# 16-bit one-hots with the keys innermost, in the counting loop of an edge sort and in the fetch of target values

## Chip, cores and metric

The program runs on one core of a Trainium2 chip. The metric is the device time of one execution in microseconds, the median of several runs. The engines named below are PE (TensorE; PEld are its weight loads), DVE (VectorE), ACT (ScalarE), POOL (GpSimd) and SP (SyncE, which here only issues transfers).

## What is computed

A stack of four graph layers over 6250 nodes and 100,000 edges, each with a residual and a layer norm. Two places matter here. The edges are sorted by their source node, and a spline convolution moves each edge's coordinates by a value fetched at its two end nodes:

```
row, col = (edge_index[0], edge_index[1])
deg = jax.ops.segment_sum(jnp.ones_like(msg[:, 0]), row, num_segments=N)
...
new_pseudo = jnp.clip(pseudo + t[col] - t[row], 0.0, 1.0)
basis2, idx2 = spline_basis(new_pseudo)
```

## The kernel before

Edges lie as 128 partitions by J = 784 columns. Each edge has a key (a node number below 6272), which is split into a low digit (key modulo 128) and a high digit (key divided by 128, below NT = 49). Gathers and counts over keys are made with one-hot matrices: for a column of 128 keys, `hot_lo` is 128 x 128 (is the low digit n?) and `hot_hi` is 128 x 49. A matmul of the two counts how many of the 128 keys equal each node number.

**stage_rank** sorts the edges. DVE first splits the keys into digits. Then come two loops of 28 iterations, two steps each.
- The counting loop (`v.Fori(0, steps)` at L402 on DVE, L502 on PE): in each of 56 steps DVE makes the one-hots of ST = 14 key columns (`make`: copy 28 digits to PSUM at L374, `hot_lo` at L377, `hot_hi` at L379), into one of two buffers, and PE adds 14 matmuls to `table` (L507) and then frees the buffer (`hot_free`).
- After a short piece on DVE (L412 to L395) the ranking loop, again of 56 steps, makes the same one-hots once more, finds each edge's place, and POOL scatters the edges to `sorted` (L564), 14 scatters for each step. DVE may overwrite the buffer `at`/`rows` only when `rank_free` has been raised, and SP raises it when it has seen that buffer's scatters land (L575).
- SP's program in this stage begins with `load_constants`: 49 transfers that clear `adj` (L279), then the loads of the weights and constants (L282). Its loop on `rank_free` stands behind these in SP's order.

**stage_targets** fetches t[col] for all edges. Steps of CH = 28 key columns, 28 steps in a loop. In each, DVE makes the one-hots of the next step (L1761, L1764, L1766), and then picks the values of this one in `units` = 7 units of 4 columns (multiply at L1777) and sums them (L1784). PE for each unit adds 4 matmuls to `counts` (L1827), turns 4 `hot_lo` into rows (L1828), ACT copies these out of PSUM (L1816), and PE looks up the values with 12 matmuls (L1838) into one of two `found` buffers, which DVE frees after its pick. POOL meanwhile works off a share of another scatter (L1086, `scatter_pairs`).

All one-hots are bf16 with the key outermost, `[P, keys, digits]`, so that the matrix of one key column is contiguous. The digits they are compared with, and the row of numbers `iota`, are f32, and the digits lie in PSUM.

## Time and profile before

| | us |
|---|---|
| median of 3 runs (12901.63 to 12932.95) | 12922.68 |
| profiled execution, its own time | 12949.96 |
| its span | 12948.2 |
| counting loop | about 44 to 256 |
| ranking loop | about 274 to 1562 |
| stage_targets, its loop | about 5481 to 6567 |

Over the span PE is busy 26%, DVE 43%, ACT 19%, POOL 52%. Such shares are means over some fifty stages that run one after another, so each stage is to be read by itself.

### The profile page before, as it was taken

How to read it: one execution, taken by the hardware profiler on the slowest of the kernel's cores; microseconds unless marked ns; L12 is line 12 of the kernel's file. 1: busy time of each engine (PE TensorE's matmuls, PEld its weight loads, DVE VectorE, ACT ScalarE, POOL GpSimd, SP SyncE). 2: the span in 40 equal slices, each digit the busy share in tenths (PEclk: the TensorE clock that was granted, in tenths of full speed). 3: DMA queues.
4: the chain of work that ended last, by engine and by line, in shares of the span. 5: the costliest groups of instructions: out<-in, count | busy, mean ns of one | idle time of the engine just before them, and what ended most of it. 6: DMA issues, size and time to landing. Idle time of an engine off the chain costs nothing. (4 is left out here: it accounts for less than half of the span.)

```text
span 12948.2 us, 84897 instructions
## 1 busy us (share of the span) xinstructions
PE 3406.5 (26%) x19713; PEld 2120.5 (16%) x19713; DVE 5568.4 (43%) x7052; ACT 2481.3 (19%) x3625; POOL 6758.2 (52%) x6784
## 2 busy tenths in 40 slices
PE   2344301773333333402410001000100010005877
PEld 1222200331111111302410001000100010004544
DVE  7333385445444445302755442222322277774111
ACT  0222143332222222100100000111111134440000
POOL 0666566006666666573047766776677656651000
PEclk9555555885555555555755555555555555557899
DMA  6000022786777777300036641111111123335899
GB/s 269 2 3 3 12 89 76 292 336 208 233 233 236 235 233 229 93 0 0 0 100 185 176 137 32 33 35 29 32 34 32 29 63 99 95 96 172 325 385 362
DMA packets 587391, 1693.59 MB, mean 131 GB/s; under 512 B 268075, under 2 KB 322770, under 8 KB 569201
## 3 DMA queue, kind: packets, MB, share of 16 engines
q0 software_dynamic: 292720, 608.23, 18.5%
q1 hardware_dynamic: 230560, 722.30, 14.4%
q10 hardware_dynamic: 63952, 361.30, 7.3%
q8 instruction: 56, 0.92, 0.0%
q14 instruction: 103, 0.84, 0.0%
HBM read 1016.07 MB, written 675.24 MB: 131 GB/s over the span
## 5 line engine op out<-in xcount | busy, mean ns | idle before, releaser
L1979 POOL DMA_INDIRECT ring<-tab_gat,at x2352 | 2350.8, 999 | 920.5 <-issue 837.5
L710 POOL DMA_INDIRECT ring<-z_stn,at x1568 | 1512.5, 965 | 1530.6 <-POOLq L707 1034.8
L710 POOL DMA_INDIRECT ring<-z_conv,at x784 | 802.0, 1023 | 890.1 <-POOLq L707 628.1
L564 POOL DMA_INDIRECT sorted<-rows,at x784 | 801.2, 1022 | 776.1 <-POOLq L562 542.8
L1503 PE MATMUL pair_acc<-pair_w,pair_cell 32*112 32x384 f32 (+1 forms) x1120 | 788.4, 881 | 1545.7 <-issue 519.8
L1086 POOL DMA_INDIRECT adj<-val_a,at_a x784 | 780.3, 995 | 334.9 <-issue 255.7
L2558 PE MATMUL acc<-spot,ones 128*128 128x128 f32 x6 | 2.3, 486 | 3440.4 <-PEq L2549 1195.5
L1253 PE MATMUL acc<-tile,parts 128*96 128x448 f16 (+1 forms) x3430 | 730.5, 362 | 254.8 <-DVE parts L1177 138.7
L1898 DVE COPY corner_banks<-w 128x56 f32 (+1 forms) x140 | 35.6, 255 | 1579.8 <-issue 448.7
L2090 DVE COPY peak<-peak 128x6 f32<-128x6 f32 x112 | 20.9, 187 | 1562.2 <-DMA ring<-tab_gat,at 1498.7
L1503 PEld LDWEIGHTS pair_acc<-pair_w,pair_cell 32*112 32x112 f32 x1120 | 315.6, 296 | 2017.4 <-issue 2017.4
L2558 PEld LDWEIGHTS acc<-spot,ones 128*128 128x128 f32 x6 | 1.5, 312 | 3441.1 <-issue 3441.1
L2126 DVE TENSOR_TENSOR_SCAN sums<-decay,sums 128x1176 f32<-128x1176 f32 (+1 forms) x112 | 517.3, 4619 | 29.0 <-issue 12.2
L1540 ACT COPY pair_block<-pair_acc 112x384 f32<-112x384 f32 (+1 forms) x896 | 380.0, 501 | 749.3 <-issue 374.5
L1253 PEld LDWEIGHTS acc<-tile,parts 128*96 128x96 bf16 (+1 forms) x3430 | 404.9, 125 | 574.3 <-DMA tile<-adj 238.4
L2014 ACT ACTIVATE weights_bank<-arg 128x168 f32<-128x168 f32 (+1 forms) x112 | 31.2, 279 | 2410.0 <-issue 1953.1
L2113 DVE TENSOR_TENSOR sums<-ring,weights_bank 128x1008 f32<-128x1008 f32 (+1 forms) x112 | 430.0, 3839 | 145.9 <-issue 109.4
L1159 POOL DMA_INDIRECT own<-tab_gcn,ex_src x5 | 5.0, 990 | 905.1 <-DMA tab_gcn<-hop 602.4
L2029 ACT COPY out_rows<-sums 128x1176 f32<-128x1176 f32 (+1 forms) x112 | 443.0, 3955 | 49.0 <-ACTq L2028 15.9
L1623 PE MATMUL planes<-wsb,turned 64*128 64x384 f32 (+1 forms) x1960 | 421.9, 537 | 72.9 <-PEq L1619 72.9
L1777 DVE TENSOR_TENSOR prod<-found,hot_hi 128x588 f32<-128x588 f32 x196 | 151.1, 771 | 622.9 <-remote 300.5
L822 DVE TENSOR_TENSOR_SCAN sums<-decay,sums 128x448 f32<-128x448 f32 (+2 forms) x168 | 387.8, 2308 | 43.2 <-issue 24.2
(503 smaller groups left out, 9709.3 us busy)
## 6 DMA issues: line engine op xcount, KB each, us to landing
tile<-adj SPq DMA_DIRECT2D x490, 784.0 KB, 21.4
z_stn<-block ACTq DMA_DIRECT2D x245, 800.0 KB, 4.9
z_conv<-pair_block ACTq DMA_DIRECT2D x224, 700.0 KB
run_gat<-out_rows SPq DMA_DIRECT2D x56, 1596.0 KB
adj<-zero SPq DMA_DIRECT2D x49, 1568.0 KB, 38.6
run_basis<-out_rows SPq DMA_DIRECT2D x28, 1750.0 KB
ring<-tab_gat,at POOLq DMA_INDIRECT x2352
run_gat<-out_rows SPq DMA_DIRECT2D x56, 672.0 KB
```

The source lines that it names most:

```text
L564: g.indirect_dma_start(out=dest, out_offset=bass.IndirectOffsetOnAxis(ap=at[b][:, k:k + 1], axis=0), in_=rows[b][:, k, :], in_offset=None) ...
L710: g.indirect_dma_start(out=view(bufs[b], k), out_offset=None, in_=table, in_offset=bass.IndirectOffsetOnAxis(ap=at[n][b][:, k:k + 1], axis ...
L822: v.tensor_tensor_scan(flat, decay[:, :, :].rearrange("p f j -> p (f j)"), flat, 0.0, ALU.mult, ALU.add).then_inc(dve_step, 1)
L1086: g.indirect_dma_start(out=adj, out_offset=bass.IndirectOffsetOnAxis(ap=at_a[:, k:k + 1], axis=0), in_=val_a[:, k:k + 1], in_offset=None). ...
L1253: ins = pe.matmul(acc[0:3 * w, b, 0:HW_B], parts[:, t_, :, :].rearrange("p k f -> p (k f)"), self.ring[n % RING][:, b * HW_B:(b + 1) * HW_ ...
L1503: last = pe.matmul(self.acc[g][0:self.nodes, n, 0:(hi - lo) * self.fo], self.cell[:, :], cols, start=True, stop=True)
L1540: last = a.copy(self.blocks[plane - slot][:, lo:hi, slot, :], self.acc[plane % 2][0:self.nodes, n, 0:(hi - lo) * self.fo].rearrange("p (u ...
L1623: ins = pe.matmul(self.acc[g][:, n, 0:(hi - lo) * self.fo], self.turned[rows, k, :], cols, start=True, stop=True)
L1979: g.indirect_dma_start(out=ring[b][:, k, :], out_offset=None, in_=tab_gat, in_offset=bass.IndirectOffsetOnAxis(ap=at[b][:, k:k + 1], axis= ...
L2029: a.copy(out_rows[b][:, :, 0:n_sums], sums[b][:, :, :, :].rearrange("p h f j -> p j (h f)"))
L2113: v.tensor_tensor(sums[b][:, :, 1:per_head, :], val_of(ring[b]), ex.unsqueeze(2).to_broadcast([P, NH, width, ch]), ALU.mult)
L2126: v.tensor_tensor_scan(flat, decay[:, :, :, :].rearrange("p h f j -> p (h f j)"), flat, 0.0, ALU.mult, ALU.add).then_inc(dve_step, 1)
```

## The change

The one-hots of the counting loop, and `hot_lo` in stage_targets, are compared from bf16 operands that both lie in SBUF, with the keys as the innermost axis: a table `number` holds each number n repeated once for each key of a step, `short` holds the digits as bf16, and the output has keys innermost. PE then reads the one-hot matrix of key column j with a step of 14 elements (counting loop, both operands) or 28 elements (stage_targets, the weights alone). The ranking loop's `make` and `hot_hi` in stage_targets stay as they were.

```diff
+                short = sb(st, "short_b", [P, 2, SW, ST], BF16)
+                number = sb(st, "number_b", [P, P, ST], BF16)
...
+                def keys_inside(tile):
+                    return tile[:, :, :].rearrange("p j k -> p (j k)").rearrange("p (k j) -> p k j", j=ST)
...
+                    v.tensor_copy(number[:, :, :], iota[:, 0:P].unsqueeze(2).to_broadcast([P, P, ST]))
...
+                    v.tensor_copy(short[:, 0, :, :].rearrange("p i s -> p s i"), digit_i[:, :].rearrange("p (s i) -> p s i", s=ST))
                     v.tensor_copy(digits[:, 0, :, 0:SW], digit_i[:, :].rearrange("p (s i) -> p s i", s=ST)).then_inc(dve_step, 1)
...
-                            make(b, it * 2 + b)
+                            v.tensor_tensor(keys_inside(hot_lo[b]), short[:, 0, bass.ds(it * 2 + b, 1), :].to_broadcast([P, P, ST]),
+                                            number[:, :, :], ALU.is_equal)
+                            v.tensor_tensor(keys_inside(hot_hi[b]), short[:, 1, bass.ds(it * 2 + b, 1), :].to_broadcast([P, NT, ST]),
+                                            number[:, 0:NT, :], ALU.is_equal).then_inc(dve_step, 1)
+                            v.wait_ge(dve_step, 1)
+                            v.sem_inc(dve_step, -1)
+                            v.sem_inc(sem("hot_made"), 1)
...
-                                last = pe.matmul(cell(table, j), hot_lo[b][:, j, :], hot_hi[b][:, j, :], start=False, stop=False)
+                                last = pe.matmul(cell(table, j), keys_inside(hot_lo[b])[:, :, j], keys_inside(hot_hi[b])[:, :, j], start=False, stop=False)
...
-                digits = sb(st, "digits", [P, 2, J + CH])
+                digits = sb(st, "digits", [P, J + CH])
+                short = sb(st, "short_b", [P, J + CH], BF16)
+                number = sb(st, "number_b", [P, P, CH], BF16)
...
-                hot_lo = [sb(st, f"hot_lo{b}", [P, CH, P], BF16) for b in range(2)]
+                hot_lo = [sb(st, f"hot_lo{b}", [P, P, CH], BF16) for b in range(2)]
...
+                    v.tensor_copy(number[:, :, :], iota[:, 0:P].unsqueeze(2).to_broadcast([P, P, CH]))
...
-                        v.tensor_copy(keys, digits[:, :, bass.ds(col, CH)]).then_inc(dve_step, 1)
-                        v.wait_ge(dve_step, 1)
-                        v.sem_inc(dve_step, -1)
-                        v.tensor_tensor(hot_lo[b][:, :, :], keys[:, 0, :].unsqueeze(2).to_broadcast([P, CH, P]),
-                                        iota[:, 0:P].unsqueeze(1).to_broadcast([P, CH, P]), ALU.is_equal)
-                        v.tensor_tensor(hot_hi[b][:, :, :], keys[:, 1, :].unsqueeze(2).to_broadcast([P, CH, NT]),
+                        v.tensor_copy(keys, digits[:, bass.ds(col, CH)]).then_inc(dve_step, 1)
+                        v.wait_ge(dve_step, 1)
+                        v.sem_inc(dve_step, -1)
+                        v.tensor_tensor(hot_lo[b][:, :, :], short[:, bass.ds(col, CH)].unsqueeze(1).to_broadcast([P, P, CH]),
+                                        number[:, :, :], ALU.is_equal)
+                        v.tensor_tensor(hot_hi[b][:, :, :], keys.unsqueeze(2).to_broadcast([P, CH, NT]),
...
-                            pe.matmul(counts_, hot_lo[b][:, k, :], hot_hi[b][:, k, :], start=False, stop=False)
-                            last = pe.matmul(turned[(b * units + u) % 2][:, j, :], hot_lo[b][:, k, :], unit[:, :], start=True, stop=True)
+                            pe.matmul(counts_, hot_lo[b][:, :, k], hot_hi[b][:, k, :], start=False, stop=False)
+                            last = pe.matmul(turned[(b * units + u) % 2][:, j, :], hot_lo[b][:, :, k], unit[:, :], start=True, stop=True)
```

The body of the counting loop on DVE, two steps, before. A row named ISA is a short instruction without a tile that stands ahead of an operation whose address depends on the loop's counter:

```order
L374 ISA [waits hot_free0]
L374 COPY keys<-digits 128x28
L377 TENSOR_TENSOR hot_lo_77<-keys,iota 128x1792 [waits dve_step]
L379 TENSOR_TENSOR hot_hi_79<-keys,iota 128x686
L374 ISA [waits dve_step,hot_free1]
L374 COPY keys<-digits 128x28
L377 TENSOR_TENSOR hot_lo_78<-keys,iota 128x1792 [waits dve_step]
L379 TENSOR_TENSOR hot_hi_80<-keys,iota 128x686
```

The same place with the change:

```order
L414 ISA [waits hot_free0]
L414 TENSOR_TENSOR hot_lo_79<-short_b,number_b 128x1792
L416 ISA
L416 TENSOR_TENSOR hot_hi_81<-short_b,number_b 128x686
L414 ISA [waits dve_step,hot_free1]
L414 TENSOR_TENSOR hot_lo_80<-short_b,number_b 128x1792
L416 ISA
L416 TENSOR_TENSOR hot_hi_82<-short_b,number_b 128x686
```

The copy to PSUM and the wait behind it are gone, and an address row now stands between the two comparisons.

In stage_targets, the end of one step's picks and the make of the next on DVE, before (`moved` is the sum of the picks):

```order
L1777 TENSOR_TENSOR prod<-found_227,hot_hi_217 128x588
L1784 ISA
L1784 TENSOR_REDUCE moved<-prod 128x84
L1761 ISA
L1761 COPY keys<-digits 128x56
L1764 TENSOR_TENSOR hot_lo_215<-keys,iota 128x3584
L1766 TENSOR_TENSOR hot_hi_217<-keys,iota 128x1372
L1777 TENSOR_TENSOR prod<-found_228,hot_hi_218 128x588
```

The same place with the change:

```order
L1795 TENSOR_TENSOR prod<-found_231,hot_hi_221 128x588
L1802 ISA
L1802 TENSOR_REDUCE moved<-prod 128x84
L1779 ISA
L1779 COPY keys<-digits 128x28
L1782 ISA
L1782 TENSOR_TENSOR hot_lo_219<-short_b,number_b 128x3584
L1784 TENSOR_TENSOR hot_hi_221<-keys,iota 128x1372
L1795 TENSOR_TENSOR prod<-found_232,hot_hi_222 128x588
```

The copy to PSUM stays, with half its elements, and `hot_lo` gets an address row of its own behind it. PE, ACT, POOL and SP keep their order in both stages.

## Rows read from the trace of the kernel before

**Rows 1.** Window: length, busy us (instructions) of PE PEld DVE ACT POOL, PEclk, DMA, GB/s

```profile
44.00:256.00 212.00, 42.57 (x788) 35.88 (x788) 168.71 (x168) 0.00 (x0) 0.00 (x0) 1.00 0.96 389
```

**Rows 2.** Timeline of two steps of the counting loop: start, us, idle before

```profile
142.29 0.21 DVE L374 COPY keys<-digits 128x28 f32 x1 [0.78 <-DVEq L405]
142.64 2.03 DVE L377 TENSOR_TENSOR hot_lo<-keys,iota 128x1792 bf16<-128x1792 f32 x1
144.59 0.86 DVE L379 TENSOR_TENSOR hot_hi<-keys,iota 128x686 bf16<-128x686 f32 x1
145.74 0.74 PE L507 MATMUL table<-hot_hi,hot_lo 128*128 128x49 bf16 x14 [3.19 <-PEq L505]
145.89 0.21 DVE L374 COPY keys<-digits 128x28 f32 x1 [0.44 <-DVEq L405]
...
149.82 0.21 DVE L374 COPY keys<-digits 128x28 f32 x1 [0.78 <-DVEq L405]
```

**Rows 3.** Instructions by form over the whole trace, DVE: busy us, mean ns

```profile
L377 DVE TENSOR_TENSOR hot_lo<-keys,iota 128x1792 bf16<-128x1792 f32 x113 | 228.8, 2024 | 16.6 <-DVEq L376 0.2
L379 DVE TENSOR_TENSOR hot_hi<-keys,iota 128x686 bf16<-128x686 f32 x113 | 97.4, 862 | 0.0
L386 DVE CAST parts<-first 128x686 bf16<-128x686 f32 x57 | 30.0, 526 | 8.3
```

**Rows 4.** Timeline around the ranking loop's start, SP (issuing) and DVE

```profile
250.89 1.08 SPq L282 DMA_DIRECT2D run_gat<-negs  x1
...
337.23 0.17 DVE L463 CAST at<-rank 128x14 int32<-128x14 f32 x1
```

**Rows 5.** DMA queues: in the counting loop's window, then 0 to 400 us

```profile
q1 hardware_dynamic: 16642, 82.47, 96.2%
...
q0 software_dynamic: 2225, 0.29, 0.7%
```

**Rows 6.** Windows of stage_targets

```profile
5500.00:6024.00 524.00, 31.65 (x197) 21.27 (x196) 17.75 (x14) 5.85 (x10) 373.91 (x373) 0.50 0.02 0
6096.00:6562.00 466.00, 228.01 (x3165) 216.48 (x3165) 350.58 (x252) 91.88 (x157) 0.00 (x0) 0.75 0.00 0
```

**Rows 7.** Timeline of one step of stage_targets, DVE and PE

```profile
6219.05 0.22 DVE L1761 COPY keys<-digits 128x56 f32 x1 [0.24 <-DVEq L1786]
6219.42 3.89 DVE L1764 TENSOR_TENSOR hot_lo<-keys,iota 128x3584 bf16<-128x3584 f32 x1
...
6225.16 0.77 DVE L1777 TENSOR_TENSOR prod<-found,hot_hi 128x588 f32<-128x588 f32 x1 [0.35 <-DVEq L1775]
6226.19 1.37 PEld L1838 LDWEIGHTS found<-parts,lo_rows 128*128 128x128 bf16 x12 [9.40 <-issue]
...
6226.28 0.77 DVE L1777 TENSOR_TENSOR prod<-found,hot_hi 128x588 f32<-128x588 f32 x1 [0.35 <-DVEq L1775]
...
6228.01 0.77 DVE L1777 TENSOR_TENSOR prod<-found,hot_hi 128x588 f32<-128x588 f32 x1 [0.96 <-DVEq L1775]
...
6230.09 0.77 DVE L1777 TENSOR_TENSOR prod<-found,hot_hi 128x588 f32<-128x588 f32 x1 [1.30 <-DVEq L1775]
...
6231.21 0.77 DVE L1777 TENSOR_TENSOR prod<-found,hot_hi 128x588 f32<-128x588 f32 x1 [0.35 <-DVEq L1775]
...
6232.49 0.77 DVE L1777 TENSOR_TENSOR prod<-found,hot_hi 128x588 f32<-128x588 f32 x1 [0.52 <-DVEq L1775]
...
6233.61 0.77 DVE L1777 TENSOR_TENSOR prod<-found,hot_hi 128x588 f32<-128x588 f32 x1 [0.35 <-DVEq L1775]
```

**Rows 8.** Windows of two steps of stage_targets

```profile
sum 40.95, PE 20.06 PEld 19.05 DVE 30.88 ACT 8.20 POOL 0.00; mean PE 10.03 PEld 9.53 DVE 15.44 ACT 4.10 POOL 0.00
```

**Rows 9.** Instructions by line on DVE, 6024 to 6562 us

```profile
L1764 DVE TENSOR_TENSOR hot_lo<-keys,iota 128x3584 bf16<-128x3584 f32 x26 | 101.2, 3891 | 3.8
```

**Rows 10.** Weight loads of line 272: ns min/median/max; operands with step 3 and step 1

```profile
L272 PEld LDWEIGHTS flip<-ident,raw_ps x21: 190/226/226, 26.3 to 31.3; 112*128 112x128 f32 x21
L272 PEld LDWEIGHTS flip<-ident,rawf_dst x7: 226/226/226, 23.9 to 25.1; 112*128 112x128 f32 x7
```

More of the change, by code:

```diff
@@ L368, in _ @@
                     v.sem_inc(dve_step, -1)
+                    v.tensor_copy(short[:, 1, :, :].rearrange("p i s -> p s i"), digit_i[:, :].rearrange("p (s i) -> p s i", s=ST))
                     v.tensor_copy(digits[:, 1, :, 0:SW], digit_i[:, :].rearrange("p (s i) -> p s i", s=ST)).then_inc(dve_step, 1)
@@ L1722, in stage_targets @@
                 moved = sb(st, "moved", [P, J, D3])
-                keys = ps(st, "keys", [P, 512])[:, 0:2 * CH].rearrange("p (s j) -> p s j", s=2)
+                keys = ps(st, "keys", [P, 512])[:, 0:CH]
                 counts_ = ps(st, "counts", [P, 512])[:, 0:NT]
@@ L1733, in _ @@
                 def _(v):
-                    v.memset(digits[:, :, J:J + CH], 0.0)
+                    v.memset(digits[:, J:J + CH], 0.0)
+                    v.memset(short[:, J:J + CH], 0.0)
+                    v.tensor_copy(number[:, :, :], iota[:, 0:P].unsqueeze(2).to_broadcast([P, P, CH]))
                     v.memset(none[:, :], 0.0)
@@ L1744, in _ @@
                     v.sem_inc(dve_step, -1)
-                    v.tensor_copy(digits[:, 0, 0:J], digit_i[:, :])
+                    v.tensor_copy(short[:, 0:J], digit_i[:, :])
                     v.tensor_copy(parts[:, 1, :, :], rest[:, :, :]).then_inc(dve_step, 1)
@@ L1752, in _ @@
                     v.sem_inc(dve_step, -1)
-                    v.tensor_copy(digits[:, 1, 0:J], digit_i[:, :])
+                    v.tensor_copy(digits[:, 0:J], digit_i[:, :])
                     v.tensor_copy(parts[:, 2, :, :], rest[:, :, :]).then_inc(dve_step, 1)
```

## The prediction

> **What bounds the kernel now.** The windows by stage come first, since both places are loops of their own. In the counting loop DVE is busy 168.71 of 212 us and PE 42.57 [rows 1]. The timeline shows the order: DVE copies the digits, compares, compares, and starts over 3.60 or 3.93 us after the copy before (142.29, 145.89, 149.82), a mean of 3.765 us; PE's 14 matmuls take 0.74 us and then it sits idle for 3 us until the next `hot_made` [rows 2]. So DVE sets the pace for 56 steps, and nothing else in the loop waits last. The transfer queue is full beside it (share 0.96 [rows 1]), but no instruction of the loop needs it.
>
> In stage_targets the windows show two regimes. From 5500 to 6024 us DVE is busy 18 of 524 us and POOL 374, while PE does about 200 matmuls in all; from 6096 PE does 3165 in 466 us and DVE is busy 75% [rows 6]. While POOL scatters, PE crawls, and a faster DVE is worth nothing. Of the 29 makes of `hot_lo`, 26 lie behind POOL's end [rows 9]; only these count. There two steps take 40.95 us, with DVE busy 15.44 in each 20.5 [rows 8]. Within a step DVE does all its work in series: keys, `hot_lo`, `hot_hi`, seven picks, the sum [rows 7]. The picks at first wait for PE: the third comes 0.96 us after DVE was free and the fourth 1.30 us, while the fourth to fifth and sixth to seventh are 1.12 us apart, which is DVE's own 0.77 plus its 0.35 wait. PE has meanwhile been idle for 9.40 us ahead of that (the row of L1838), so a shorter make has slack there.
>
> **Counting loop.** No row shows a comparison of two 16-bit operands from SBUF. Its bounds are no gain, 2.02 us, and half the time for each element. The two forms of today give 2024 ns for 1792 elements and 862 for 686 [rows 3]: 1.05 ns for an element and 0.14 us fixed. That the engine can pass two elements in that time is shown only for a one-source cast: 686 elements in 526 ns [rows 3], against 862 for the comparison. I take the halved time, since the new operands and output are all 16-bit and contiguous innermost: `hot_lo` 0.14 + 0.94 = 1.08 us, `hot_hi` 0.14 + 0.36 = 0.50, together 1.50 with today's overlap of 0.08. The copy (0.21) and its 0.15 wait go. The gap ahead of a step stays at 0.44 or 0.78, mean 0.61 [rows 2]. The added address row between the comparisons costs from nothing (it can pass while `hot_lo` runs) to 0.24, today's gap ahead of the copy at L1761 that has both a wait and such a row [rows 7]; I take 0.1. A step is then 1.50 + 0.61 + 0.1 = 2.2 us, and 56 steps save 56 x (3.765 - 2.2) = 88 us.
>
> Ahead of the loop DVE now builds `number` (1792 elements: 1.1 us at the cast's pace, 2.0 at the comparison's) and two `short` (784 elements each, 0.5 to 1.0 by the same two paces): 2.1 to 4.0 us, taken as 3.
>
> What is late next: the ranking loop starts 85 us sooner. DVE's third step there needs SP to have raised `rank_free`, and SP reaches that loop only when `load_constants` has been issued, at 250.89 + 1.08 = 252.0 us. Today the third step stores its places at 337.2, long after; less 85 that is 252.2 [rows 4], a tie. Scatters now share the queues with the clearing: 28 scatters come before the third step. The 70 scatters up to 400 us made 2225 packets, and the clearing's 16642 packets took 96% of 212 us on 16 engines, or 0.20 us each [rows 5]. If each of 28 x 32 packets waited out one of those, that is 56 for each engine, 11 us. At least nothing; I take 3. The counting part is 88 - 3 - 3 = 82 us (bounds 68 to 90).
>
> **stage_targets.** `hot_lo` goes from 3.89 to 0.14 + 1.88 = 2.02 us, the keys copy stays at about 0.2, and the address row behind a wait costs 0.1 (0.24 against 0.15). That is 1.77 us a step, 26 x 1.77 = 46 us. The setup (`number`, 3584 elements, 2.0 to 3.9 us) delays PE's start by less than 3 us, ahead of the stretch that POOL's end closes, so it is hidden; were that cover gone it would cost those 3. Against the 46 stand two things on PE. First its clock: averaged over the steps it is 0.75, half the time at 1.2 GHz and half at 2.4 [rows 6]. The waits of 0.96 and 1.30 fall at the low level after the long idle, and the later picks at the high one. If the rise comes later, three spacings of 1.12, 1.28 and 1.12 turn into 2.08 each, 2.7 us a step more; if the idle time of 9.4 us, now 7.6, no longer drops the clock, the spacings of 1.73 and 2.08 shrink by 1.4. Second, the weights that PE reads with a step. For both I take 0.4 us a step, nearer the row of today than either end: 10 us. The stage gives 36 us.
>
> **Sum.** 82 + 36 = 118 us. The profiled execution would take 12950 - 118 = 12832; it lies 27 us above the median of the runs, so from the median it is 12923 - 118 = 12805 us.
>
> **Rivals.**
>
> (a) Slower: PE becomes the bound. The one-hots are now read with a step of 28 or 56 bytes. In the counting loop PE passes one load and matmul in 0.04 us ((0.74 - 0.22)/13). With X us for each, a step needs 14X + 0.3 us (the 0.3 is from the end of `hot_hi`, 144.59 + 0.86, to PE's start at 145.74 [rows 2]), and up to X = 0.13 all of it is hidden behind DVE. In stage_targets 24 loads of a step stand between picks (the `turn` of the last three units), and cost up to 24(X - 0.04) there. The saving of both stages is then 56 x (3.765 - 0.3 - 14X) - 6 + 26 x (1.77 - 24(X - 0.04)), which is zero at X = 0.18 us. The dearest load at hand, f32 at line 272, takes 226 ns [rows 10]; at that price the kernel loses 59 us: 12982. Against it: line 272 reads `raw_ps` with a step of 12 bytes and `rawf_dst` with 4, at the same 226 ns. A step of 12 bytes is not one of 28, so this speaks only weakly. Chance 0.05, with 0.08 for a milder form (X of 0.12 to 0.18) that takes the gain of stage_targets and some of the other: by the same formula 12845 to 12920.
>
> The Trainium skill (Advanced Engine Details and Errata, SBUF Cachelines) says that SBUF lines hold 16 bytes and that at least two hits on a line are needed to hide its latency; steps of 28 and 56 bytes never hit twice, which by that rule is rival (a). The equal loads of line 272, with 1.3 hits a line, do not show such a penalty. The Trainium skill (TensorE: Matmul & The Clock Gate, Weight-path perf modes) says that a fast weight load takes its columns packed or strided, which speaks the other way; no run here shows that.
>
> (b) The comparison doesn't run at two elements a step. Then the counting loop saves the copy and its wait less the address row, 0.26 x 56 = 15 us, less 3 of setup, and stage_targets loses 0.1 x 26: 9 us in all, 12914. For it: no two-source row in the trace is at that pace. Chance 0.08. The Trainium skill (VectorE: DVE Perf Modes, the perf-mode tier table) gives `tensor_tensor` twice the rate for bf16 in SBUF and the plain rate for anything in PSUM; no row of this trace has such operands, so it bears on the chance alone.
>
> (c) PE's clock in stage_targets stays low through the picks: 118 - 36 = 82, plus 46 - 26 x 2.7 = -24, leaves 58 us: 12865. For it: PE idles just before them. Chance 0.08. (d) It stays high: 82 + 46 + 26 x 1.4 = 164 us: 12759. For it: the idle time shrinks. Chance 0.07.
>
> (e) The collision at the third ranking step costs its full 11 us: 12813, within the forecast's own range.
>
> **How the numbers follow.** The forecast has a chance of 0.64, with 12775 to 12845 as its own range. To leave out no more than 2 in 10, the range goes down to (d) and up through (c) and most of the milder (a): 12750 to 12880. Left out are (b), the full (a) and the tails. A measurement tells 0.3%, about 39 us. Faster by more: the forecast, (c), (d) and most of the milder (a), 0.85. Within: (b) and the rest, 0.10. Slower: (a), 0.05.
>
> **What would show it.** In the profile after: `hot_lo` of 1792 elements near 1.08 us and of 3584 near 2.02; steps of the counting loop 2.2 us apart, its end near 170 us; the third ranking step stored near 252 us, with a wait on SP's `rank_free` if (e) is right; PE's loads at L507's successor still near 0.04 apart; steps of stage_targets near 19.1 us. The prediction is wrong if those loads are 0.13 us or more apart, if the comparisons keep 2.02 and 3.89 us, or if the picks wait longer than today.

## The result, and the profile after

The changed kernel took 12833 us (median of 6 runs, 12820 to 12864); the kernel before, measured beside it, 12932 us (6 runs, 12902 to 12979). The ratio is 0.9926, with a 95% interval from 0.9913 to 0.9939: 99 us gained (79 to 112 by the interval), where 118 had been forecast. The profiled execution after took 12826.38 us, 124 us less than the one before. Some 25 us of that difference arise between the end of the ranking loop and the start of the fetch, in stages that the change doesn't touch (3896 us from the last scatter of the one to the first of the other before, 3870 after), so the medians are the better measure and the two traces are compared stage by stage.

Windows of the changed kernel, with the columns of [rows 1]: the counting loop, then stage_targets while POOL scatters and after it (compare [rows 6]).

```profile
50.00:172.00 122.00, 84.14 (x788) 72.88 (x788) 85.03 (x112) 0.00 (x0) 0.00 (x0) 1.00 1.01 424
...
5410.00:5934.00 524.00, 30.75 (x200) 23.66 (x200) 15.86 (x14) 5.86 (x10) 376.89 (x376) 0.50 0.02 0
6010.00:6440.00 430.00, 252.28 (x3139) 243.78 (x3137) 300.43 (x245) 91.57 (x157) 0.00 (x0) 0.79 0.00 0
```

The counting loop now takes 122 us instead of 212, and PE, which does the same 788 matmuls, is busy twice as long. Its timeline shows why (compare [rows 2]):

```profile
99.41 1.09 DVE L414 TENSOR_TENSOR hot_lo<-short_b,number_b 128x1792 bf16<-128x1792 bf16 x1 [0.46 <-DVEq L413]
100.42 0.51 DVE L416 TENSOR_TENSOR hot_hi<-short_b,number_b 128x686 bf16<-128x686 bf16 x1
101.23 1.49 PE L521 MATMUL table<-hot_hi,hot_lo 128*128 128x49 bf16 x14 [0.50 <-PEq L519]
101.72 1.09 DVE L414 TENSOR_TENSOR hot_lo<-short_b,number_b 128x1792 bf16<-128x1792 bf16 x1 [0.79 <-DVEq L413]
...
103.70 1.09 DVE L414 TENSOR_TENSOR hot_lo<-short_b,number_b 128x1792 bf16<-128x1792 bf16 x1 [0.46 <-DVEq L413]
```

The steps come 2.31 and 1.98 us apart, a mean of 2.15. The gaps ahead of a step are those of before (0.46 and 0.79), and the address row between the comparisons costs nothing. PE's 14 matmuls take 1.49 us instead of 0.74: (1.49 - 0.27)/13 = 0.094 us for each pair of load and matmul, where it was 0.04. PE still has 0.50 us of idle time ahead of a burst in the shorter steps, so all of this is hidden.

The instructions by line, over 44 to 172 us, give the comparisons and one of the two casts that fill `short` (columns as in [rows 3]):

```profile
L414 DVE TENSOR_TENSOR hot_lo<-short_b,number_b 128x1792 bf16<-128x1792 bf16 x56 | 61.2, 1093 | 35.1 <-DVEq L413 35.1
L416 DVE TENSOR_TENSOR hot_hi<-short_b,number_b 128x686 bf16<-128x686 bf16 x56 | 28.5, 509 | 0.0
...
L369 DVE CAST short_b<-digit_i 128x784 bf16<-128x784 int32 x1 | 1.9, 1857 | 0.1
```

At the third step of the ranking loop DVE waits, and what it waits for is on SP. The timeline of SP's last constant load and of DVE's places, third and fifth step (compare [rows 4]):

```profile
256.72 1.06 SPq L282 DMA_DIRECT2D run_gat<-negs  x1
...
258.39 0.22 DVE L475 COPY rows<-payload 128x112 f32 x1 [4.66 <-DVEq L474]
...
310.82 0.22 DVE L475 COPY rows<-payload 128x112 f32 x1 [0.47 <-DVEq L474]
```

One step of the fetch, with the high clock's part at its end (compare [rows 7]):

```profile
6137.06 0.19 DVE L1779 COPY keys<-digits 128x28 f32 x1 [0.63 <-DVEq L1804]
6137.49 2.03 DVE L1782 TENSOR_TENSOR hot_lo<-short_b,number_b 128x3584 bf16<-128x3584 bf16 x1 [0.23 <-DVEq L1781]
6139.43 1.58 DVE L1784 TENSOR_TENSOR hot_hi<-keys,iota 128x1372 bf16<-128x1372 f32 x1
...
6142.43 1.64 PE L1856 MATMUL found<-parts,lo_rows 128*128 128x147 bf16 x12 [7.32 <-PEq L1853]
...
6144.22 0.77 DVE L1795 TENSOR_TENSOR prod<-found,hot_hi 128x588 f32<-128x588 f32 x1 [0.96 <-DVEq L1793]
...
6146.41 0.77 DVE L1795 TENSOR_TENSOR prod<-found,hot_hi 128x588 f32<-128x588 f32 x1 [1.42 <-DVEq L1793]
...
6147.84 0.77 DVE L1795 TENSOR_TENSOR prod<-found,hot_hi 128x588 f32<-128x588 f32 x1 [0.66 <-DVEq L1793]
...
6149.12 0.77 DVE L1795 TENSOR_TENSOR prod<-found,hot_hi 128x588 f32<-128x588 f32 x1 [0.52 <-DVEq L1793]
...
6150.41 0.77 DVE L1795 TENSOR_TENSOR prod<-found,hot_hi 128x588 f32<-128x588 f32 x1 [0.51 <-DVEq L1793]
```

`hot_lo` has gone from 3.89 to 2.03 us. The picks wait longer than before: the third as long (0.96 us), the fourth 1.42 us instead of 1.30, the last three 0.66, 0.52 and 0.51 instead of 0.35, 0.52 and 0.35. The granted clock is at the low level for the first of these (0.51 from 6142.4 to 6147.0 us) and at the high one for the last (1.00 from 6147.0 to 6156.4). Over the last 20 steps all waits ahead of picks come to 4.77 us a step, where they were 4.13. The mean over the last 20 steps (from sum to sum, L1802) is 19.32 us a step, where it was 20.48.

So far, from the two traces: the counting loop ends 84 us sooner, the ranking loop gives back part of that, and the fetch gains 26 x 1.16 = 30 us.

### The profile page after: what moved, and what is told of

The parts are those of the page before. It is cut to its first block and busy times, and to the rows that moved or that the text cites. A ratio compares the mean times of both kernels' runs of the same rounds, so it can differ in the third digit from the quotient of the medians.

```text
span 12824.6 us, 84874 instructions
## 1 busy us (share of the span) xinstructions
PE 3493.7 (27%) x19713; PEld 2186.6 (17%) x19713; DVE 5436.1 (42%) x7001; ACT 2482.3 (19%) x3625; POOL 6756.2 (53%) x6784
## 3 DMA queue, kind: packets, MB, share of 16 engines
q0 software_dynamic: 292720, 608.23, 18.6%
```

## The experiments

The first two groups of runs met the program at another level: there the kernel before took 11466 and 11470 us, and in the last group 13015 us, although one chip served the second group and the last. The result, with 12932 us before, is near the last group. So only ratios within a group are compared; the section on the hardware says what differs.

### Each part alone

`counting_only` has stage_rank of the changed kernel and stage_targets of the one before, `fetch_only` the reverse.

> The change in the counting loop alone; stage_targets is the kernel before. Theory T (the parts add up, and the ranking loop gives back some 15 us because its third step waits for SP and the pattern of scatters shifts): 84 us gained at the end of the counting loop, 67 to 70 at the end of the ranking loop, and nothing after it that belongs to the change: 12932 - 68 = 12864 us, hot_lo 1.09 us, steps 2.15 us apart. Rival R (an earlier start also makes the unchanged stages from 1570 to 5300 us shorter, by the 24 us that the two profiled executions differ there): 12932 - 68 - 24 = 12840 us, and the trace has that gain between 3000 and 5300 us again. Rival F (my forecast as it stood, only 3 us given back): 12932 - 82 = 12850 us.

> The change in stage_targets alone; the counting loop is the kernel before. Theory T: the stage gains 31 us by itself, whatever came before it: 12932 - 31 = 12901 us; the sum of this and of the counting part alone is then the whole gain of 99. Rival F (my forecast): 36 us, 12896. Rival S (the gain of stage_targets depends on where the stage starts against POOL's scatters, which the earlier stages shifted): less than 20 us, over 12912.

Measured: `counting_only` 11398 us, ratio 0.9939 (0.9925 to 0.9953), 69 us; `fetch_only` 11433 us, ratio 0.9970 (0.9960 to 0.9981), 34 us; the kernel before 11466 us. These are theory T's numbers: 69 + 34 = 103 us for the sum, and 84 us at the end of the counting loop became 70 at the end of the ranking loop (the last scatter starts at 1265.03 instead of 1334.71). Of rival R nothing is seen: from the last scatter of the ranking loop to the first of the fetch, unchanged stages, `counting_only` takes 3566 us and `fetch_only` 3544, so its lead shrinks there; `fetch_packed`, with the same ranking loop as `counting_only`, takes 3544 too, so such differences belong to the execution. My own 82 us (rival F) lie 13 us off the median but within the interval (54 to 86 us); what speaks against them is the trace, with its 70 us at the end of the ranking loop. For `fetch_only` the interval (22 to 46 us) holds both T and F.

The timelines of `counting_only` show where the ranking loop gives back. SP's last constant load, DVE's third step, POOL's:

```profile
255.85 1.08 SPq L282 DMA_DIRECT2D run_gat<-negs  x1
...
257.54 0.22 DVE L475 COPY rows<-payload 128x112 f32 x1 [27.62 <-DVEq L474]
...
258.78 0.96 POOL L578 DMA_INDIRECT sorted<-rows,at  x1 [16.74 <-POOLq L576]
```

In this group POOL works without a pause, one step of 14 scatters each 18.6 us, so DVE is ready for the third step at 230 us (257.54 less 27.62) and then stands for 27.6 us until SP is through with `load_constants`. POOL runs dry for 16.7 us. Since POOL is what paces the loop there, that is never made up: the ranking loop takes 1059 us from first to last scatter, and 1043 in `fetch_only`.

### The changed kernel in the second group

> The changed kernel once more, on the chip of this group of runs. The two parts alone gained 70 us (ratio 0.9939) and 34 us (0.9970) where the kernel before took 11466 us. Theory T (the parts add up): 104 us, a ratio of 0.9909. Rival D (the parts get in each other's way, since the fetch then starts at another moment of POOL's scatter): less than 90 us, a ratio above 0.9922.

Measured: 11361 us against 11470, ratio 0.9905 (0.9888 to 0.9921). The parts add up (0.9909 from their product).

### Keys outermost, 16 bits

```diff
-                            v.tensor_tensor(keys_inside(hot_lo[b]), short[:, 0, bass.ds(it * 2 + b, 1), :].to_broadcast([P, P, ST]),
-                                            number[:, :, :], ALU.is_equal)
+                            v.tensor_tensor(hot_lo[b][:, :, :], short[:, 0, bass.ds(it * 2 + b, 1), :].rearrange("p i s -> p s i").to_broadcast([P, ST, P]),
+                                            number[:, :].unsqueeze(1).to_broadcast([P, ST, P]), ALU.is_equal)
```

The same for the other comparisons of 16-bit operands, with PE's operands contiguous.

> Both places compare 16-bit operands that lie in SBUF, as in the changed kernel, but with the digits innermost as before: the digit of the key is repeated along the innermost axis (a step of zero) and PE reads contiguous matrices. Theory T (the double pace needs the keys innermost, so that no operand repeats along the innermost axis): hot_lo stays near 2.02 us for 1792 and 3.89 for 3584 elements, and only the copy to PSUM with its wait is saved in the counting loop, (0.21 + 0.15 - 0.1) x 56 = 15 us: 12932 - 15 + 3 for the setup + nothing in stage_targets = 12920 us. Rival B (16-bit operands in SBUF are enough): 1.09 and 2.02 us as in the changed kernel, PE's pair back at 0.04 us: 12833 - 10 for PE in stage_targets = 12823 us or less.

Measured: 11472 us, ratio 1.0003 (0.9994 to 1.0012). By line, over 100 to 240 us:

```profile
L414 DVE TENSOR_TENSOR hot_lo<-short_b,number_b 128x1792 bf16<-128x1792 bf16 x41 | 83.0, 2025 | 25.5 <-DVEq L413 25.5
```

With an operand repeated along the innermost axis the comparison runs at the old pace, so 16-bit operands in SBUF alone bring no double pace; the layout is needed. (Whether the layout would bring anything with 32-bit operands, no run shows.) At the end of the ranking loop the kernel was 16 us ahead of `fetch_only`, which has that loop as before (last scatter at 1318.88 and 1334.71 us), near the 12 that theory T has. In the fetch it lost 19: from the first scatter of that stage to the next stage it takes 610 us, and `counting_only` 591. It came out 5 us behind, and neither theory had that. The cause is on POOL. The timeline of the fetch in this kernel:

```profile
5122.13 3.89 DVE L1782 TENSOR_TENSOR hot_lo<-short_b,number_b 128x3584 bf16<-128x3584 bf16 x1 [0.23 <-DVEq L1781]
5122.98 3.88 POOL L1100 DMA_INDIRECT adj<-val_a,at_a  x1 [0.30 <-issue]
```

and of the changed kernel (`after_again`):

```profile
5122.84 2.02 DVE L1782 TENSOR_TENSOR hot_lo<-short_b,number_b 128x3584 bf16<-128x3584 bf16 x1 [0.23 <-DVEq L1781]
5123.44 2.26 POOL L1100 DMA_INDIRECT adj<-val_a,at_a  x1 [0.30 <-issue]
```

A scatter that begins while the new comparison runs does not end until 0.8 us after the comparison has ended (5122.84 + 2.02 = 5124.86, and 5125.70), where an undisturbed one takes 0.97 us in all. So it is under all 29 comparisons of both kernels: the scatter ends 0.84 or 0.85 us after the comparison, whenever it began. POOL's 392 scatters of the stage, by line, in `counting_only` (comparison of before), `after_again` and `outer16`, one row of each:

```profile
L1100 POOL DMA_INDIRECT adj<-val_a,at_a x392 | 380.4, 970 | 143.6 <-issue 127.3 <-SPq L1724 16.4
```

```profile
L1100 POOL DMA_INDIRECT adj<-val_a,at_a x392 | 420.1, 1072 | 143.6 <-issue 127.2 <-SPq L1724 16.4
```

```profile
L1100 POOL DMA_INDIRECT adj<-val_a,at_a x392 | 476.2, 1215 | 143.7 <-issue 127.2 <-SPq L1724 16.5
```

The burst grows by 40 and by 96 us, for 29 comparisons of 2.02 (59 us) and of 3.89 (113 us). In `outer16` it ends after DVE's loop, and the next stage waits for it. The Trainium skill (SBUF — State Buffer, Who interferes with whom) has a rule for this: a VectorE instruction with two SBUF inputs contends with a GpSimd instruction that reads SBUF, and whoever issues first has the shared ports for the whole instruction. The trace agrees (the scatters read their places from SBUF), and the comparison at the plain pace shows that the double pace isn't needed for it. The same section says that a probe had not seen `tensor_tensor` stall a transfer; here it does, by 1.3 to 2.9 us for the two scatters above. The kernel before read its digits from PSUM, and its 970 ns are undisturbed. I had not weighed this. It speaks against the change, and what it costs depends on whether POOL or DVE ends the stage.

### PE's part in the fetch

```diff
+                    def packed(b, k):
+                        return hot_lo[b][:, :, :].rearrange("p n k -> p (n k)")[:, k * P:(k + 1) * P]
...
-                            pe.matmul(counts_, hot_lo[b][:, :, k], hot_hi[b][:, k, :], start=False, stop=False)
+                            pe.matmul(counts_, packed(b, k), hot_hi[b][:, k, :], start=False, stop=False)
```

The matmul into `turned` likewise. The kernel leaves out the right matrices: what PE reads is contiguous but is not the one-hot matrix of a key column, so the values are wrong and only the times can be used.

> The changed kernel, but in stage_targets PE reads 128 contiguous elements of hot_lo for each key column where the changed kernel reads them with a step of 28 elements. The matrix is then the wrong one (the fetched values and the counts are not the true ones), the work of every engine is the same. Theory T (the step costs PE): at the high clock a pair of counts and turned goes back from 0.13 to 0.084 us, picks 5 to 7 from 1.29 to 1.12 us apart, and the 26 steps gain 0.3 to 0.5 us each, 8 to 13 in all: 12833 - 10 = 12823 us. Rival N (the loss of 0.4 us a step is the clock, which rises later after a shorter idle time, and the step costs nothing): the granted clock stays 0.79, the picks stay 1.29 apart, 12833 us.

Measured: 11350 us, ratio 0.9901 (0.9886 to 0.9916), 117 us below before; the two parts alone sum to 103. The mean step is 18.77 us, and 19.37 in `after_again`. Weight loads by line, `after_again` and then `fetch_packed`:

```profile
L1845 PEld LDWEIGHTS counts<-hot_hi,hot_lo 128*128 128x128 bf16 x580 | 80.2, 164 | 0.0
L1846 PEld LDWEIGHTS turned<-unit_b,hot_lo 128*128 128x128 bf16 x580 | 79.2, 154 | 0.0
```

```profile
L1849 PEld LDWEIGHTS turned<-unit_b,hot_lo 128*128 128x128 bf16 x616 | 60.3, 107 | 0.0
L1848 PEld LDWEIGHTS counts<-hot_hi,hot_lo 128*128 128x128 bf16 x616 | 58.6, 103 | 0.0
```

Reading with a step of 28 elements costs 0.60 us in each step of the fetch. That is theory T. Rival N is out: the granted clock is not higher with packed matrices but lower (0.77 against 0.80 from 4900 to 5300 us), and the steps are shorter all the same. They are 20.48 - 18.77 = 1.71 us shorter than before, nearly all of the 1.77 that DVE's work was to save. Of the 0.60 us the stage keeps only a part: it ends here with POOL's last scatter, 7.8 us after DVE is done.

### Half of the clearing issued by ACT

```diff
-            for t_ in range(NT):
+            for t_ in range(0, NT, 2):
                 q.dma_start(adj_rows[:, t_, 0:NP], zero16[:, :]).then_inc(sem("adj_cleared"), 16)
...
+                    for t_ in range(1, NT, 2):
+                        a.dma_start(adj_rows[:, t_, 0:NP], zero16[:, :]).then_inc(sem("adj_cleared"), 16)
                     with a.Fori(0, steps):
```

> The changed kernel, but every second of the 49 transfers that clear adj is issued by ACT ahead of its ranking loop and not by SP in load_constants, so that SP reaches the loop that raises rank_free long before the third ranking step. Theory Q (the ranking loop gives back 15 us because DVE's third step waits for SP behind load_constants and the order of the work shifts from there): load_constants has been issued before 200 us, no wait at the third step, the end of the ranking loop comes 10 to 15 us sooner than in the changed kernel. Rival P (what is given back is POOL's pace: it starts 85 us sooner but its first scatters share the queues with the clearing, or its loop is the bound and starts with the same lag whatever SP does): the clearing itself takes as long, nothing is gained, within 3 us of the changed kernel. Rival W (ACT stands in its transfer issues when PE's first turned rows are ready, and the loop starts later): 5 us or more slower.

Measured: 11363 us, ratio 0.9901 (0.9885 to 0.9918), as the changed kernel. The timeline shows that the experiment did not do what it was for:

```profile
255.12 1.06 SPq L282 DMA_DIRECT2D run_gat<-negs  x1
...
256.79 0.22 DVE L475 COPY rows<-payload 128x112 f32 x1 [25.99 <-DVEq L474]
```

SP issued only 25 of the 49 transfers and was through hardly sooner (256.2 us, and 257.5 in `after_again`). The same bytes keep the transfer engines full (DMA share 1.01 from 60 to 200 us). The run says nothing for or against theory Q; it suggests that SP is held by the bytes and not by the number of its own issues, which would be so if its issues wait for room in the queues.

### The clearing inside SP's loop

```diff
-            for t_ in range(NT):
-                q.dma_start(adj_rows[:, t_, 0:NP], zero16[:, :]).then_inc(sem("adj_cleared"), 16)
...
-                    with sp.Fori(0, steps) as it:
-                        for b in range(2):
-                            sp.wait_ge(c[b].sem, it * (16 * ST) + (16 * ST + base[b]))
-                            sp.sem_inc(sem(f"rank_free{b}"), 1)
+                    for n in range(steps * 2):
+                        b = n % 2
+                        sp.wait_ge(c[b].sem, n // 2 * (16 * ST) + (16 * ST + base[b]))
+                        sp.sem_inc(sem(f"rank_free{b}"), 1)
+                        if n < NT:
+                            sp.dma_start(adj_rows[:, n, 0:NP], zero16[:, :]).then_inc(sem("adj_cleared"), 16)
```

> The changed kernel, but SP issues the 49 clearing transfers one by one inside its loop that raises rank_free (one after each raise) and not ahead of it. Moving half of them to ACT had not freed SP: its last constant load was still issued at 256, since the same bytes filled the queues. Theory Q (DVE's third ranking step waits 28 us, from 230 to 258, for SP, which stands behind the clearing; POOL then paces the loop at 18.6 us a step, so what is lost there is never made up): the third step stores its places near 238, when the first step's scatters have landed, and the end of the ranking loop comes 15 us sooner, at 1261 where the changed kernel had 1276; 11361 - 15 = 11346 us, a ratio of 0.989. Rival P (the scatters and POOL's pace suffer from transfers beside them): a step takes longer than 18.6 us; with 0.3 us more for each of 56 the 15 us are gone. Rival H (the stage's end waits for the clearing or the constants): the gain in the ranking loop is seen and lost before the next stage.

Measured, in the last group: 12900 us against 13015, ratio 0.9917 (0.9901 to 0.9933). SP's last constant load comes early, and the wait at the third step is gone:

```profile
69.18 1.03 SPq L280 DMA_DIRECT2D run_gat<-negs  x1
...
252.38 0.22 DVE L473 COPY rows<-payload 128x112 f32 x1 [0.48 <-DVEq L472]
```

So theory Q is right about what DVE waited for, and the loads that are issued until 257 us behind the clearing are issued by 70 without it. What it is worth was not seen. This group ran at the level at which DVE gets to the third step late (252 us here, and the 238 of the theory did not come), so that only the 4.66 us of the changed kernel were to be had. And the ranking loop is no measure there: from first to last scatter it takes 1289 and 1374 us in two executions of the kernel before, 1306 in the changed kernel, 1338 here. 15 us don't show in that.

### The port, with 32-bit operands

```diff
-                        v.tensor_copy(keys, digits[:, :, bass.ds(col, CH)]).then_inc(dve_step, 1)
-                        v.wait_ge(dve_step, 1)
-                        v.sem_inc(dve_step, -1)
-                        v.tensor_tensor(hot_lo[b][:, :, :], keys[:, 0, :].unsqueeze(2).to_broadcast([P, CH, P]),
+                        v.tensor_tensor(hot_lo[b][:, :, :], digits[:, 0, bass.ds(col, CH)].unsqueeze(2).to_broadcast([P, CH, P]),
```

`hot_hi` likewise, from `digits[:, 1, ...]`.

> The kernel before, but in the fetch the digits are not copied to PSUM: both comparisons read f32 digits and f32 numbers, both from SBUF, with the digits innermost. Nothing is 16-bit but the output. Theory G (VectorE holds a port that POOL's scatters need as long as it reads two operands from SBUF, whatever their type and pace; the Trainium skill, GpSimd (Pool) engine and SBUF pages, says so of two-port operations): POOL's scatters grow from 0.97 to over 1.2 us, since 28 x (3.89 + 1.58) = 153 us of its burst fall under such comparisons (109 us had added 95 in the run with 16-bit digits innermost), the burst of 392 goes from 507 to about 640 us and ends after DVE's loop, and the kernel is some 90 us slower than before although the copy is gone. Rival B (it is the 16-bit compare that holds POOL up): scatters stay at 0.97 us, and the kernel gains 0.3 us x 28 = 8 us.

Measured: 13020 us against 13015, ratio 1.0003 (0.9993 to 1.0013). Both times missed. At the level of this group POOL's burst is over before DVE's loop gets going (as in [rows 6]), so there was little for a port to hold up. But three makes of `hot_lo` do fall under the burst, and they decide the question. The first one, here:

```profile
5549.01 3.89 DVE L1760 TENSOR_TENSOR hot_lo<-digits,iota 128x3584 bf16<-128x3584 f32 x1 [0.33 <-DVEq L1755]
5549.67 4.07 POOL L1086 DMA_INDIRECT adj<-val_a,at_a  x1 [0.30 <-issue]
```

and in `before_again`, the kernel before:

```profile
5572.02 3.89 DVE L1764 TENSOR_TENSOR hot_lo<-keys,iota 128x3584 bf16<-128x3584 f32 x1
5572.31 0.97 POOL L1086 DMA_INDIRECT adj<-val_a,at_a  x1 [0.30 <-issue]
```

The scatter ends 0.84 us after the comparison, as with 16-bit operands. Under the other two makes one scatter each takes 4.02 and 3.50 us, and the mean of the 392 is 1.021 us where `before_again` has 0.997. The two comparisons differ only in where the digits lie. So theory G is right in its mechanism, for two 32-bit operands too, and rival B falls; its 90 us did not come because only 3 of the 29 makes met the burst.

The saved copy is worth nothing in the later steps: over the last 20 a step takes 20.48 us here as in `before_again`, though the make is 0.36 us shorter. The picks' waits for PE take it up (4.49 us a step, and 4.13). A shorter make does not shorten this loop one for one.

> The kernel before, for a trace from a chip like that of the experiments. Both theories of POOL's pace in the fetch (see the run sbuf32) expect POOL's scatters at 0.97 us there and the burst of 392 in 507 us, as in the run with the change in the counting loop alone, and steps of the ranking loop 18.6 us apart from the second on.

The trace of the kernel before from this group (13026 us) shows neither: the expectation was made for the other level. Its fetch has the two regimes of [rows 6] again.

### Blocks of keys innermost

```diff
-                hot_lo = [sb(st, f"hot_lo{b}", [P, P, CH], BF16) for b in range(2)]
+                hot_lo = [sb(st, f"hot_lo{b}", [P, units, P, UN], BF16) for b in range(2)]
...
-                        v.tensor_tensor(hot_lo[b][:, :, :], short[:, bass.ds(col, CH)].unsqueeze(1).to_broadcast([P, P, CH]),
-                                        number[:, :, :], ALU.is_equal)
+                        v.tensor_tensor(hot_lo[b][:, :, :, :], short[:, bass.ds(col, CH)].rearrange("p (g j) -> p g j", j=UN).unsqueeze(2).to_broadcast([P, units, P, UN]),
+                                        number[:, :, :].unsqueeze(1).to_broadcast([P, units, P, UN]), ALU.is_equal)
```

> The changed kernel, but the keys that lie innermost come in blocks: two key columns in the counting loop, four in the fetch, with the digits next and the block outermost. PE then reads with a step of 4 bytes (counting, both operands) and 8 bytes (fetch, the weights) where it had 28 and 56, and number has 256 and 512 elements where it had 1792 and 3584. Theory T (PE's cost comes from the step; a compare keeps its double pace as long as the innermost run holds pairs): hot_lo stays 1.09 and 2.02 us, PE's pair in the counting loop falls from 0.094 to about 0.04 us, the fetch gains up to 13 us as the one with packed matrices did, and 1 us of setup goes: 10 to 15 us faster than the changed kernel. Rival K (any step above 2 bytes costs PE the same): nothing but the setup, 1 to 3 us. Rival L (a short innermost run costs DVE its double pace, or some time for each run): hot_lo above 1.09 and 2.02 us; at the plain pace the whole gain of the change is lost, 11460 us.

Measured: 11350 us against 11361 for the changed kernel of the same group, ratio 0.9901 (0.9884 to 0.9917) to the kernel before. The counting loop has blocks of two keys in the same way. One step of it in `blocks`:

```profile
99.14 0.51 DVE L417 TENSOR_TENSOR hot_hi<-short_b,number_b 128x686 bf16<-128x686 bf16 x1
99.95 0.74 PE L523 MATMUL table<-hot_hi,hot_lo 128*128 128x49 bf16 x14 [1.24 <-PEq L521]
```

DVE keeps its double pace with runs of only two keys (0.51 us for `hot_hi`, 1.09 for `hot_lo`; in the fetch, with runs of four, 2.03), and PE is back at 0.74 us for 14 pairs. The fetch takes 18.77 us a step, as with packed matrices, although a weight load at a step of 8 bytes is a little longer (120 ns, and 103 to 108 contiguous, from 4900 to 5300 us). Theory T is right in each duration, and both rivals fall. The Trainium skill (Advanced Engine Details and Errata, SBUF Cachelines) wants two hits on a 16-byte line: steps of 4 and 8 bytes have them, steps of 28 and 56 bytes don't. The trace agrees in the main: 4 bytes cost nothing, 8 bytes some 15 ns a load, 56 bytes some 50 ns a load, and 28 bytes on both operands 0.054 us a pair.

### All together

> All that seems to help, together: blocks in both places, hot_hi of the fetch compared in 16 bits with keys innermost too (no digits in PSUM, no copy), half of the clearing issued by ACT, and the two casts to short written contiguously. Theory T: against the changed kernel hot_hi of the fetch goes from 1.58 to 0.14 + 0.72 = 0.86 us and the keys copy of 0.19 with its wait of 0.15 goes, 1.0 us x 26 = 26 us in the fetch; 10 to 13 from the blocks, up to 15 from the clearing, 2 from the casts: 50 us faster than the changed kernel, a ratio of 0.986 to 0.987 to the kernel before. Rival P (PE is now what the fetch waits for): the picks wait longer by what the make got shorter, and the hot_hi part gives less than 8 us. Rival M (the pick that reads hot_hi with a step of 8 bytes is slower than 0.77 us): each of the 196 picks by more than 0.1 us takes all of it back.

> The changed kernel with blocks of two and four keys innermost, the clearing inside SP's loop and the two casts to short written contiguously; hot_hi of the fetch stays as it is, since with its compare from two SBUF operands the fetch ended with POOL's burst and gained nothing. Theory T: 15 us from the clearing, 2 from the casts, 10 from the blocks (DVE's loop of the fetch then ends with POOL's burst): 11361 - 27 = 11334 us, a ratio of 0.988. Rival P (POOL's burst, 545 us from the start of the fetch, is already the end of that stage in the changed kernel): the blocks give 3 us or less, 11341 us.

Measured: `combo` 11366 us, ratio 0.9902 (0.9886 to 0.9919), no better than the changed kernel of its group; `best` 12904 us against 13015, ratio 0.9905 (0.9890 to 0.9920), and `clear_in_loop` beside it 0.9917. In `combo` the step of the fetch is down to 17.92 us, and still nothing comes of it. The timeline of DVE and POOL at the end of the stage:

```profile
5343.70 0.20 DVE L1821 COPY deg_d<-counts 128x49 f32<-128x49 f32 x1
5381.07 0.18 DVE L628 TENSOR_SCALAR has<-deg_d 128x49 f32<-128x49 f32 x1
...
5373.55 0.97 POOL L1104 DMA_INDIRECT adj<-val_a,at_a  x1 [0.30 <-issue]
```

DVE is done at 5343.9 and the next stage begins at 5381, when POOL's last scatter has landed. In `blocks` that wait is 7.8 us, in `after_again` 1.0. This is rival P of `best`, which has POOL's burst as the end of the stage: the comparisons that made DVE faster also lengthened the burst from 507 us from first to last scatter in `counting_only` to 546 in `after_again` and in `combo`, and the two ends have met. For `best` itself this was not tested, since its group ran at the other level, where the burst ends 530 us before DVE's loop. No version beats the changed kernel by more than the measurement tells.

## Why the prediction was right, and where its numbers were off

- **The comparison at two elements a step: right.** 1.08, 0.50 and 2.02 us were forecast, 1.09, 0.51 and 2.03 measured. Rival (b) is out, and `outer16` shows what it would have looked like.
- **The counting loop's step: right.** 2.15 us for 2.2; 56 steps save 90 us for 88. The address row's 0.1 was nothing.
- **The setup: too small.** 3 us forecast, 4.4 measured (from the stage's first row on DVE to the loop it takes 9.3 us instead of 4.9; the row itself came 1.6 us later in this execution). The two casts to `short` were bounded at 0.5 to 1.0 us each and took 1.86: they write with a step of 28 bytes, which I did not price.
- **The third ranking step: right at the level of the result, wrong at the other.** "Less 85 that is 252.2" says when DVE gets there. In the trace of the result DVE was ready at 253.7 us (258.39 less 4.66) and SP free at 257.8, later than the 252.0 of the sum: a wait of 4.66 us for the 3 taken. The ranking loop as a whole gave back 17.6 us in that pair of traces, but executions at that level differ by more in this loop, so no run shows that the wait cost more than itself. At the other level the step "less 85" fails: it took DVE's pace of before, and with POOL pacing the loop at 18.6 us a step DVE is ready at 230 us. The wait is then 28 us and the loop 16 us longer. The bound of 11 us was made from packets waiting in the queues, and the cause is SP's place behind `load_constants`.
- **The fetch: mechanism right, one term small.** Of 1.77 us a step 1.16 came: the 0.4 us taken for PE's clock and strided weights together measured 0.61, of which packed matrices give back 0.60 (`fetch_packed`), so the clock took nothing that shows. 30 us instead of 36. That the rest of the make's 1.77 us went through is not a matter of course: the 0.36 us of `sbuf32` did not.
- **The sum.** 84 at the end of the counting loop, less 15 in the ranking loop, plus 30 is 99 us, the measured difference of the medians. To the microsecond this is luck: the 15 are from the other level, and the interval is 79 to 112 us. Of the 28 us between 12805 forecast and 12833 measured, 19 are gain that didn't come and 9 the median of the kernel before, 12923 in the runs that the forecast started from and 12932 beside the changed kernel.
- **The signs.** The comparisons, the steps (2.15 and 19.3 us) and the end of the counting loop (172 us) came near what was named. Two others did not: PE's pairs are 0.094 us apart and not 0.04, and the picks do wait longer than before (4.77 us a step, and 4.13), which the prediction had named as a sign of being wrong. It is the strided weights, a cost that the sum had, too small: with packed matrices the waits are 4.23 us a step.
- **The rivals.** (a) was half right: PE's pair went to 0.094 us, below the 0.13 up to which the counting loop hides it. (c) and (d) did not come. The rival that I did not have is the port: the new comparisons stretch POOL's scatters. It was harmless in the runs of the result, where 3 of the 29 comparisons met POOL's burst and lengthened it by 5 us (520 to 526), well before DVE's end, and takes part of what is to be had at the other level.

## What to carry to other kernels

The comparison of two 16-bit tiles ran at double pace only where no operand repeats along the innermost axis; blocks of two to four innermost were enough for that, and keep PE's reads at steps of 4 or 8 bytes, which cost nothing or little here, while 28 and 56 cost more. (Other operations than this comparison were not tried.) Before an operand is moved from PSUM to SBUF, look at whether POOL issues indirect transfers at that time, and which of the two engines ends the stage. When a loop is made faster, ask for each later wait when its releaser is free in absolute time (here SP at 257 us, behind transfers), and not only how late the waiting engine was before.

## What the runs showed of the hardware

**Two levels of one program.** The kernel before took 11470 us in one group and 13015 us in a later one, on the same chip. The difference is in how other engines fare while POOL issues indirect scatters. The fetch of `counting_only` (the kernel before in this stage) at the first level, and of `before_again` at the second, windows:

```profile
4860.00:5340.00 480.00, 230.94 (x3224) 219.33 (x3225) 362.85 (x259) 94.36 (x161) 358.29 (x370) 0.75 0.02 0
```

```profile
5760.00:6100.00 340.00, 20.33 (x128) 13.75 (x128) 14.67 (x10) 3.52 (x6) 245.69 (x243) 0.50 0.02 0
6150.00:6600.00 450.00, 221.00 (x3080) 209.86 (x3080) 338.78 (x242) 90.26 (x154) 0.00 (x0) 0.75 0.00 0
```

At the first level PE does 3224 matmuls while POOL scatters 370 times; at the second 128 while POOL scatters 243 times, and only goes on when POOL has ended. The ranking loop shows it too: 1043 to 1063 us in all eight executions of the first level, 1289 to 1376 in the six of the second, with steps of 24, 20 and 31 us where the first has 18.6. POOL's scatters themselves take 1.02 us in that loop at both. I had read the crawl of PE as a property of the chip; it is one of a level, and its cause stays open.

**A store with a large step is dear for a cast.** 784 elements from int32 to bf16 took 1.86 us with a step of 28 bytes on the output. In `best` the same cast writes contiguously and has its step on the input:

```profile
L367 DVE CAST short_b<-digit_i 128x784 bf16<-128x784 int32 x1 | 0.9, 872 | 0.1
```

**Two SBUF operands of a comparison hold up POOL's scatters.** A scatter begun under such a comparison ended 0.84 us after it, whatever the type and the pace: 2.26 us under one of 2.02, 3.88 under one of 3.89 (16-bit), 4.07 under one of 3.89 (32-bit). With the digits in PSUM it took 0.97 us.

**Transfers ahead of it hold an issuing engine.** SP came free at 256 to 258 us whether it issued 49 transfers of 1568 KB ahead of its constant loads or 25 of them with 24 on ACT, and at 70 us where none stood ahead.
